# Flamingo-style block pair on one core: ScalarE order and clip in the first attention, one block from the experts to the last product, load order at the second attention

## The reference, cut to what matters

```python
x = x + tanh(g_xattn[0]) * L0_attention(layernorm(x), ctx)   # 16 heads of 16, 77 keys, scores clipped to +-10000
x = x + tanh(g_ffn[0])   * L0_experts(layernorm(x))          # 8 experts, the best 2 of each row, gelu
x = x + tanh(g_xattn[1]) * L1_attention(layernorm(x), ctx)   # 16 heads of 64, 77 keys
x = x + tanh(g_ffn[1])   * L1_ffn(layernorm(x))              # weights rounded to 8 bits, activations to 16
```

## Time and profile before

| what | value |
|---|---|
| median of 3 executions | 1214.83 us |
| the profiled execution | 1218.13 us |
| its span | 1216.3 us |
| mean granted TensorE clock | 0.959 |
| TensorE busy, matmul | 1061.2 us, 87% |
| VectorE busy | 907.1 us, 75% |
| ScalarE busy | 849.1 us, 70% |
| GpSimd busy | 519.1 us, 43% |

### The profile page before, as it was taken

The page is one execution under the profiler, slowest core; times in us unless marked ns, Lnnn a source line. Parts: engine busy times, 40 slices in busy tenths (PEclk is TensorE's granted clock), DMA queues, the critical chain, the costliest instruction groups (busy, mean ns, idle before and its releaser), DMA issues. The chain is left out here.

```text
span 1216.3 us, 26248 instructions
## 1 busy us (share of the span) xinstructions
PE 1061.2 (87%) x8873; PEld 778.1 (64%) x8919; DVE 907.1 (75%) x1934; ACT 849.1 (70%) x2413; POOL 519.1 (43%) x508
## 2 busy tenths in 40 slices
PE   5878777777884999999999999749999999779798
PEld 3656556654443777777777777527777777545476
DVE  3988898857635577766666667549999999679798
ACT  3888888864673555665566667548888888459897
POOL 3777777753044122212222111058888888400000
PEclk9899999997996999999999999979999999979899
DMA  5353333218963242333333334244242423000134
GB/s 126 91 129 96 111 103 116 92 40 276 257 179 109 66 99 89 94 116 118 108 119 116 120 108 156 94 163 132 84 138 82 131 89 93 26 1 1 35 113 131
DMA packets 128815, 132.13 MB, mean 109 GB/s; under 512 B 24792, under 2 KB 112973, under 8 KB 128557
## 3 DMA queue, kind: packets, MB, share of 16 engines
q1 hardware_dynamic: 119901, 112.17, 30.4%
q0 software_dynamic: 6480, 17.70, 5.3%
q10 hardware_dynamic: 2304, 0.59, 0.2%
HBM read 82.78 MB, written 47.64 MB: 107 GB/s over the span
## 5 line engine op out<-in xcount | busy, mean ns | idle before, releaser
L1536 ACT ACTIVATE exp_h<-exp_ps_h,exp_b_now 128x256 f32<-128x256 f32 (+1 forms) x320 | 124.4, 439 | 145.1 <-PE exp_ps_h L1473 141.0
L1437 POOL DMA_INDIRECT exp_xg<-xn,all_token_of x71 | 83.2, 1172 | 307.1 <-PE exp_ps_x L1452 292.0
L1473 PE MATMUL exp_ps_h<-exp_xhi,exp_w_now 128*128 128x256 bf16 (+1 forms) x1280 | 197.5, 264 | 7.3 <-DVE exp_xlo L1566 7.3
L1918 ACT ACTIVATE a_z<-a_ps_sc,a_nmx 128x77 f32<-128x77 f32 x512 | 159.2, 368 | 33.7 <-DVE a_nmx L2020 33.7
L1473 PE MATMUL exp_ps_h<-exp_xlo,exp_w_now 128*128 128x256 bf16 (+1 forms) x640 | 162.0, 264 | 0.0
L1641 DVE TENSOR_TENSOR exp_hlo<-exp_h,exp_hhi 128x512 bf16<-128x512 f32 (+1 forms) x160 | 99.2, 632 | 72.3 <-ACT exp_hhi L1540 70.6
L1473 PEld LDWEIGHTS exp_ps_h<-exp_xhi,exp_w_now 128*128 128x128 bf16 x1280 | 120.8, 99 | 22.6 <-issue 9.6
L1486 PE MATMUL exp_ps_y<-moe_w2s,exp_hhi 128*128 x529 | 125.8, 380 | 3.4 <-DVE exp_y L1658 1.3
L1918 ACT ACTIVATION_READ_ACCUMULATOR a_z<-a_ps_sc,a_nmx 128x1 f32 x512 | 128.1, 250 | 0.0
L1885 PE MATMUL a_ps_o<-a_v_now,a_phi 128*128 128x256 bf16 (+1 forms) x640 | 106.6, 273 | 2.3 <-DVE a_plo L2009 2.3
L1869 PE MATMUL a_ps_sc<-a_k_now,a_xhi 128*128 128x462 bf16 (+1 forms) x384 | 98.1, 340 | 2.4 <-DVE a_xlo L1967 2.4
(11 more groups left out here) (269 smaller groups left out, 2680.8 us busy)
## 6 DMA issues: line engine op xcount, KB each, us to landing
a_stage<-in_L_ffn_W_dram SPq DMA_DIRECT2D x64, 256.0 KB, 3.2
y_slots<-exp_y SPq DMA_DIRECT2D x71, 128.0 KB, 1.7
fold_k<-route_kst SPq DMA_DIRECT2D x16, 308.0 KB, 4.3
fold_v<-route_vst SPq DMA_DIRECT2D x16, 308.0 KB
exp_job_in<-fold_k SPq DMA_DIRECT2D x14, 352.0 KB, 3.3
exp_job_in<-fold_v SPq DMA_DIRECT2D x14, 352.0 KB, 3.2
a_x<-in_x_dram SPq DMA_DIRECT2D x32, 128.0 KB, 2.3
x<-a_xo SPq DMA_DIRECT2D x32, 128.0 KB, 1.7
```

The lines of the kernel that those rows point to most:

```text
L1437: pool.indirect_dma_start(out=xg[:, v, u, :], out_offset=None, in_=xn_dram[:, :], in_offset=bass.IndirectOffsetOnAxis(ap=at.bitcast(U32), ...
L1473: mm = pe.matmul(hidden[:, i, f % 2, slots(j)], w1_now[:, v, k, hl, f * P:(f + 1) * P], xx[:, k, slots(j)], start=(q == 0), stop=(q == len ...
L1536: ins = act.activation(h[:, f, slots(j)], hidden[:, i, f % 2, slots(j)], ACT.Gelu_apprx_tanh, bias=b1_now[:, v, f:f + 1])
L1918: ins = act.activation(z[:, u, h * KEYS:(h + 1) * KEYS], ps_sc[:, j, (h - SB[j][0]) * KEYS:(h - SB[j][0] + 1) * KEYS], ACT.Exp, bias=nmx[: ...
```

## The change

1. First attention. ScalarE's `normal(T+1)` moves from behind the Exp to the head of the slot, between `a_attnT` and `a_qT`. VectorE computes the `shift` one slot earlier, of T+2 and behind the maxima of T. The clip of the 16 maxima is a scalar_tensor_tensor against a tensor `limit` that is set once.
2. The clearing of the semaphores moves from in front of the second attention to between the first attention and the routing.
3. Experts, second attention, and both parts of the ffn are written into one block, so that the engines don't meet between them; explicit waits take its place.
4. Second attention's start: rows of tile 0, then a wait for the gathers of tile 0, keys, rows of tile 1, biases, rows of 2 and 3; the values wait for `x2_done` of 2. GpSimd does the power of tile 0 before the gathers of tile 2.
5. Ffn: a one-column Gelu ahead of the waits, on ScalarE. Rows for `f3` are loaded once eight halves are rounded. The eight store semaphores become two.

```diff
@@ first attention, ScalarE's slot
+                if has(T + 1):
+                    normal(T + 1, 1 - u, (t + 1) % RING)
                 if has(T):
                     act.wait_ge(s["q_done"], T + 1)
...
                     act.activation(zt, zt, ACT.Exp, scale=-scale).then_inc(s["exp_done"], 1)
-                if has(T + 1):
-                    normal(T + 1, 1 - u, (t + 1) % RING)
@@ first attention, VectorE
             block_keys(0)
+            ln_shift(1, 1)
+            dve.memset(limit[:, :], CLAMP / scale).then_inc(s["limit_set"], 1)
+            dve.wait_ge(s["limit_set"], 1)
...
-                if has(T + 1):
-                    ln(T + 1, (t + 1) % 2, (t + 1) % RING)
...
+                if has(T + 2):
+                    ln_shift(T + 2, u)
                 if has(T - 1):
                     sums(T - 1, (t - 1) % 2)
                 if has(T):
                     dve.wait_ge(s["max_done"], T + 1)
-                    dve.tensor_scalar(mx[:, :], mx[:, :], -CLAMP / scale, CLAMP / scale, ALU.max,
-                                      ALU.min).then_inc(s["mx_done"], 1)
+                    dve.scalar_tensor_tensor(out=mx[:, :], in0=mx[:, :], scalar=-CLAMP / scale,
+                                             in1=limit[:, 0:1].broadcast_to((P, HEADS)), op0=ALU.max,
+                                             op1=ALU.min).then_inc(s["mx_done"], 1)
@@ experts, second attention, f1, f3
-        block = ctx.enter_context(nc.Block())
+        block = C.block
@@ second attention, SyncE
-            for r in range(2):
-                load(r, r)
+            load(0, 0)
+            for c in range(TOPK):
+                sp.wait_ge(gathered[0][c], 16)
+            load_keys(0)
+            load(1, 1)
...
-            load_keys(0)
-            sp.wait_ge(s["x2_done"], 1)
+            sp.wait_ge(s["x2_done"], 2)
             load_values(0)
@@ second attention, GpSimd
-            for T in range(3):
-                gather(T, T, 0)
+            gather(0, 0, 0)
+            gather(1, 1, 0)
             power(0, 0)
+            gather(2, 2, 0)
@@ f1
+                dve.wait_ge(C.attended["amax_done"], TILES)
...
+                pe.wait_ge(C.attended["w_loaded"], 48)
...
+                act.activation(warm[:, :], C.half[:, 0:1], ACT.Gelu)
                 act.wait_ge(s["step"], 5)
+                for stored in C.attended_stored:
+                    act.wait_ge(stored, 16 * TILES // 2)
+                act.wait_ge(C.attended["w_loaded"], 48)
@@ f3, SyncE
+                sp.wait_ge(C.rounded, 2 * 4)
                 load(0, 0)
@@ program
             attention(nc, C, x_dram, x1_dram, w0, 0, split, v_dram)
+            clear_semaphores(nc, C)
...
             routing(nc, C, x1_dram, xn_dram, io["L0_ffn_Wg"], w1, folded)
+            C.block = ctx.enter_context(nc.Block())
...
-        clear_semaphores(nc, C)
```

More of the change, by code:

```diff
@@ L198, in attention @@
         shift = m.sb("shift", [P, 2])
+        limit = m.sb("limit", [P, 1])
         xn = m.sb("xn", [P, D])
@@ L227, in attention @@
                  "zc_done", "exp_done", "sum_done", "rsum_done", "norm_done", "turned_p", "pT_done", "pv_done",
-                 "attn_done", "o_done", "xo_done", "xb_done", "mask_step", "kmask_done", "hi_done", "lo_done")
+                 "attn_done", "o_done", "xo_done", "xb_done", "mask_step", "kmask_done", "limit_set", "hi_done", "lo_done")
         s = {n: m.sem(n) for n in names}
@@ L574, in ln_mean, with ln_shift @@
                 dve.tensor_scalar(veps[:, u:u + 1], mv[:, u, 1:2], EPS, None, ALU.add).then_inc(s["veps_done"], 1)
-            def ln(T, u, r):
+            def ln_shift(T, u):
                 dve.wait_ge(s["rstd_done"], T + 1)
@@ L621, in _ @@
             ln_mean(0, 0)
-            ln(0, 0, 0)
+            ln_shift(0, 0)
             ln_stats(1, 1, 1, 0)
@@ L1315, in experts @@
         C.slots_stored = stored
-        for sem in stored:
-            C.sems.remove(sem)
-        block = ctx.enter_context(nc.Block())
+        block = C.block
         def run(eng, step):
@@ L1714, in folded_attention @@
         full = [(0, 0, 4, P), (1, 4, 8, P), (2, 8, RCH - 1, P), (2, RCH - 1, RCH, ROWS - (RCH - 1) * P)]
-        block = ctx.enter_context(nc.Block())
+        C.attended, C.attended_stored = s, x_stored
+        block = C.block
         def run(eng, slot):
@@ L2087, in ffn @@
             tmp = m.sb("tmp", [P, 2])
+            warm = m.sb("warm", [P, 1])
             x_scale = m.sb("x_scale", [P, 2])
@@ L2096, in ffn @@
             s = {n: m.sem(n) for n in names}
-            block = ctx.enter_context(nc.Block())
+            C.rounded = s["rounded"]
+            block = C.block
             def run(eng, step):
@@ L2233, in ffn @@
             x_in = [m.sem(f"x_in{i}") for i in range(2)]
-            stored = [[m.sem(f"stored{v}_{r}") for r in range(G)] for v in range(2)]
-            block = ctx.enter_context(nc.Block())
+            stored = [m.sem(f"stored{v}") for v in range(2)]
+            block = C.block
             x3_v = x3_dram.rearrange("(g r p) d -> g p r d", r=G, p=P)
@@ L2267, in step @@
                             sp.wait_ge(s["y_done"], (g - 1) * G + r + 1)
-                            sp.dma_start(out_dram[(g - 1) * GT + r * P:(g - 1) * GT + (r + 1) * P, :], y[:, 1 - v, r, :]).then_inc(stored[1 - v][r], 16)
+                            sp.dma_start(out_dram[(g - 1) * GT + r * P:(g - 1) * GT + (r + 1) * P, :], y[:, 1 - v, r, :]).then_inc(stored[1 - v], 16)
                         if has(g + 1):
@@ L2273, in _ @@
                 for v in range(2):
-                    for r in range(G):
-                        sp.wait_ge(stored[v][r], 16 * NG // 2)
+                    sp.wait_ge(stored[v], 16 * G * NG // 2)
             @block.scalar
@@ L2328, in residual @@
                     if has(g - 2):
-                        dve.wait_ge(stored[w][r], 16 * (n - 1))
+                        dve.wait_ge(stored[w], 16 * G * (n - 1))
                     dve.scalar_tensor_tensor(out=y[:, w, r, :], in0=ps[:, w, r, 0:D], scalar=C.gate[:, 3:4],
```

## The result

The changed kernel takes **1185.10 us** (median of four executions, 1184.02 to 1186.12) against 1214.24 us for the kernel before in the same comparison (1213.11 to 1215.24): ratio 0.9746, 95% interval 0.9725 to 0.9768 (the quotient of the two medians is 0.9760, inside the interval). The forecast was 1191.5 us with a range from 1185.0. The profiled execution took 1185.41 us, its span is 1183.6 us; between the two profiled executions the spans differ by 32.7 us.

| from ... to ... | before, us | after, us | difference |
|---|---|---|---|
| query copy of tile 0 ...

A forecast was written before the change was run, and what follows sets the result against it. It took the first attention's slot loop, including the normalised rows, and waits at the second attention's start and end as bounds. −14.7 + 1.3 − 4.7 − 5.2 = −23.3 us from 1214.83 gave 1191.5 us, range 1185 to 1201.

The forecast's parts named there:

- Normalisation moved: First attention: normalised rows leave the slot's loop, 0.49 us in each of 30 periods, 14.7 us less (bounds nothing, 17.7).
- `shift` earlier and clip: First attention, VectorE: `shift` a slot earlier and the clip against `limit` were each to give nothing.
- case B: First attention: the clip falls behind GpSimd's division and waits 2.25 us for it; 1238 us, chance 0.04.
- Clearing: Semaphores cleared between first attention and routing: 1.3 us more there (bounds 0.3 and 1.6).
- Start of the second attention: Without clearing and meeting, gathers start sooner with the queue to themselves: first maxima 4.7 us earlier (bounds 2 and 7).
- One block: End of the second attention: VectorE no longer waits for GpSimd's drain before the ffn, 5.2 us less (bounds 3.6, 5.4).
- Meeting between f1 and f3, table load, stores: Ffn: the meeting and earlier Gelu table load are small and counted as nothing; merged store semaphores give nothing.
- A: First attention: the move frees nothing, the 0.49 us only changes its place; 1206.2 us, chance 0.13 with halves.
- C: Start of the second attention: keys land as late as before and nothing is won there; 1196 us, chance 0.12.

The follow-up runs named there:

- the filled kernel: The changed kernel with the normalisation back behind Exp and six overwritten transposes on TensorE before its wait for the row: 1201.50 us, ratio 0.9885.
- the unfilled: The changed kernel with the normalisation put back behind Exp on ScalarE, all else as changed: 1206.42 us, ratio 0.9917.

## Where the prediction failed, and what of it held

The prediction had the direction and the mechanism of each part right, and the other terms within 1 us, and the term for the moved normalisation, its largest, wrong: 14.7 us, with bounds of nothing and 17.7, where the two traces have 18.97 and the move alone measured 20.6 by the medians. That is past the term's own upper bound, and it makes the sum 5.8 us too small. By its steps:

- **Normalisation moved**, -14.7: the step that failed. The row's place in the loop was priced rightly: 28 of the 30 periods are 13.6 us shorter together, 0.49 each, not counting the long slots' excess, and the filled kernel and the change differ by 14.8 us. What failed is that "there are 30 periods; each has one such step": it takes TensorE's clock as the same before and after and puts its part at nothing. The text says that the transpose of the next rows then "waits for nothing and moves ahead", and makes no term of it. Behind these waits (29.0 us in 29 times) the clock fell in three slots of that trace. In the traces before and after this is 3.0 us in two long slots, and 2.0 us in the slot from tile 1 to 2 beyond its 0.49; against it the slot from tile 2 to 3 came out 7.61 us long instead of 6.96, for which no run gives a cause. Between the unfilled and the filled kernel the clock's part is 7.1 us. The long slots were in the trace of before: 226.73 / 30 is 7.56, and the forecast took 7.45.
- **`shift` earlier and clip**, 0: right, and for the reason given: both forms wait for GpSimd, and the new loop takes the wait away from both. The margin to case B is 0.17 us, as thin as the prediction puts it. The Trainium skill's page "SBUF — State Buffer", section "SBUF: two separate sides", says that a VectorE operation with two SBUF inputs and a GpSimd operation that reads SBUF hold one port pair exclusively. The new clip's 540 ns with GpSimd at work and 110 without agree with it.
- **Clearing**, +1.3: measured +0.84 behind the first attention. At its old place it cost 1.5, where it was counted in the next step.
- **Start of the second attention**, -4.7: measured -5.67 against the first profile, -4.1 against the kernel with only the normalisation moved (19.98 us to 15.89). The chain was right link by link: first gather 2.41 us behind the last expert row (the forecast's 788.3 is 3.2, so it was 0.8 us too cautious), landed in 4.08 (4.0), keys in 6.1 (6 to 7), maxima 13.48 behind the first gather (13.7).
- **One block**, -5.2: measured -5.30. Putting the meeting back costs 5.9.
- **Meeting between f1 and f3, table load, stores**, 0: 0.3 together, in one pair of traces; none of them was tried alone.

The sum again, with the median of the kernel that has the move alone and the other terms from traces: 20.6 us, less 0.8 for the clearing, 4.1 and 5.3 for the two places, makes 29.2; measured 29.1. That it meets so closely is in part luck, since the executions of one kernel differ by 2 us and more (the kernel before, by 9 us in the last comparison). Of the rivals, A needed slots of 7.45, B a clip behind the division, C an unchanged start; the rows above show none of them.

## What to carry to other kernels

An idle wait of TensorE inside a loop can have two prices: the wait, if it is on the loop, and the clock of what follows. Compare the mean period with the commonest one before multiplying; where they differ, look at the granted clock of the long ones. And before an engine meeting is priced, read every sequencer's drain there, GpSimd's above all, and how long that engine had been free.

## What the runs showed of the hardware that was not expected

- TensorE's clock fell in three slots and in tile 2's slot with the row behind Exp, and in none when six idle transposes, 0.82 us together, stood in the 0.96 us wait, at the same 7.45 us pace. With the change TensorE still waits 1.26 us in each slot, for `a_pT`, and the clock stayed at 1.00 from 30 to 234 us in all eleven profiles with the row at the head. Why that wait is harmless and the two shorter ones (0.96 and 0.56 us) aren't always is open.
- GpSimd's drain took 6.6 to 7.5 us at the end of each block in which it had issued gathers (6.6 where that was the second attention alone, 7.15 and more with the experts in it), 2.15 and 2.35 us at the end of the routing and of the first attention, and 0.04 us right behind another drain. That the gathers cause it is the reading that fits these blocks; no kernel was made to tell it apart.
- Filling TensorE's idle time ahead of a stage is no safe gain: in front of the second attention it raised the clock, and the time was that of the change, in front of the ffn it spread the times over 6.6 us.
